# Finer waits, later weight loads, bf16 bound matmuls and a split last block in a transformer layer on 8 cores

## The reference

```python
lat = rmsnorm(x @ wkv_a_w.T, norm_w)
kv = lat @ wkv_b_w.T                     # k, v, split by heads; q = x @ wq_w.T
scores = jnp.einsum('bqhd,bkhd->bhqk', q, k) * scale      # causal mask
o = jnp.einsum('bhqk,bkhd->bqhd', softmax(scores), v)
return o @ out_w.T + out_b
```

## Time and profile before

| | us |
|---|---|
| runs of the kernel | 1611.94, 1614.55, 1836.63 (median 1614.55) |
| the profiled execution | 1611.35 |
| its slowest core, first to last instruction | 1609.5 |
| its quickest core | 1601.5 |

### The profile page before, as it was taken

How to read it: one execution, slowest core, us unless ns; L and a number is a source line. 1 busy time by engine, 2 the same in 40 slices (tenths; PEclk the granted TensorE clock), 3 DMA queues, 4 the chain that set the end, 5 groups by cost and what they waited for, 6 DMA issues and landing times.

```text
span 1609.5 us, 22614 instructions; the slowest of 8 cores (1601.5 to 1609.5 us)
## 1 busy us (share of the span) xinstructions
PE 1562.8 (97%) x8698; PEld 760.1 (47%) x8698; DVE 440.6 (27%) x996; ACT 363.4 (23%) x480; POOL 82.1 (5%) x174
## 2 busy tenths in 40 slices
PE   3999999999989999999999999999999999999998
PEld 2644555555554444444444444444444444444444
DVE  5735444444445662111111111011111111111111
ACT  3854565656652001101111001111011000000000
POOL 1210100000000000000000000000000000000000
PEclk8999999999999999999999999999999999999999
DMA  9853445222447975344653645473532283939110
GB/s 274 285 96 77 72 80 87 44 34 41 72 67 106 234 210 120 32 42 37 53 52 32 61 41 51 40 62 31 42 37 27 21 111 60 123 53 128 55 53 27
DMA packets 75607, 127.59 MB, mean 79 GB/s; under 512 B 46128, under 2 KB 48496, under 8 KB 70768
## 3 DMA queue, kind: packets, MB, share of 16 engines
q0 software_dynamic: 17856, 58.73, 35.5%
q1 hardware_dynamic: 57648, 67.42, 15.0%
HBM read 233.08 MB, written 16.78 MB: 155 GB/s over the span
## 4 chain that ended last, share of the span: by engine, by line
PE 92%; DMA 5%; DVE 1%; issue 1%; ACT 0%; POOL 0%; SPq 0%; DVEq 0%; ACTq 0%; POOLq 0%
PE PS L1324 21%; PE PS L1302 21%; PE PS L1308 21%; PE PS L1096 7%; PE PS L1284 4%; PE PS L1177 4%; PE PS L1153 4%; PE PS L1105 3%; PE PS L1115 3%; PE PS L1060 3%; DMA RES<-xq 2%; DMA WST<-wkva 1%; DMA OT<-ONa 1%; DMA X<-xq 1%; PE PS L1124 1%
## 5 line engine op out<-in xcount | busy, mean ns | idle before, releaser
L1302 PE MATMUL PS<-X2T,W 128*128 128x512 bf16 x1536 | 347.2, 379 | 0.0
L1308 PE MATMUL PS<-X2T,W 128*128 128x512 bf16 x1536 | 347.2, 379 | 0.0
L1308 PEld LDWEIGHTS PS<-X2T,W 128*128 128x128 fp8e4 x1536 | 150.3, 98 | 181.2
L1302 PEld LDWEIGHTS PS<-X2T,W 128*128 128x128 fp8e4 x1536 | 150.3, 98 | 181.2
L864 DVE SCALAR_TENSOR_TENSOR FUSE<-PS,CF,SIL 128x512 bf16<-128x512 f32 x96 | 72.1, 751 | 587.4 <-PE PS L1308 587.4
L1015 ACT ACTIVATE SIL<-PS,CF 128x512 bf16<-128x512 f32 x96 | 66.0, 687 | 589.7 <-PE PS L1302 589.6
L940 ACT ACTIVATE P<-PS,NEGB 128x1024 bf16<-128x1024 f32 x192 | 169.8, 899 | 124.8 <-PE PS L1153 115.7
L1324 PE MATMUL PS<-WDa,FUSE 128*128 128x512 fp8e4 x768 | 166.1, 379 | 0.0
L1324 PE MATMUL PS<-WDb,FUSE 128*128 128x512 fp8e4 x768 | 166.1, 379 | 0.0
L1324 PEld LDWEIGHTS PS<-WDa,FUSE 128*128 128x128 bf16 x768 | 75.1, 98 | 90.6
L1324 PEld LDWEIGHTS PS<-WDb,FUSE 128*128 128x128 bf16 x768 | 75.1, 98 | 90.6
(11 more groups left out here) (123 smaller groups left out, 956.4 us busy)
## 6 DMA issues: line engine op xcount, KB each, us to landing
W<-gu POOLq DMA_DIRECT2D x48, 512.0 KB, 8.3
WQ<-wq POOLq DMA_DIRECT2D x16, 512.0 KB, 6.6
X<-xo SPq DMA_DIRECT2D x8, 1024.0 KB, 9.1
WO<-wo POOLq DMA_DIRECT2D x16, 512.0 KB, 11.2
RES<-xq SPq DMA_DIRECT2D x8, 1024.0 KB, 6.8
res_scr<-RES SPq DMA_DIRECT2D x8, 1024.0 KB, 8.7
RB<-res_scr SPq DMA_DIRECT2D x32, 256.0 KB, 4.9
out<-OB SPq DMA_DIRECT2D x32, 256.0 KB, 2.5
```

The costliest lines, as they stand in the source:

```text
L1302: mm = e.matmul(bank(ffn_bank(f)), W8[io % 4][:, c * 128:(c + 1) * 128], X2T[:, c * 1024 + qb * 512:c * 1024 + qb * 512 + 512], start=(c = ...
L1308: mm = e.matmul(bank(ffn_bank(f) + 1), W8[io % 4][:, 2048 + c * 128:2048 + (c + 1) * 128], X2T[:, c * 1024 + qb * 512:c * 1024 + qb * 512 ...
```

## The change

1. P's waits for transposed heads: the first chunk waits for head 12 (208) instead of head 14 (240); chunks 13, 14 and 15 then wait for their own head.
2. W8[i], i = 0 to 3, waits for v_add of 8 + 4 i, that is for the adds of tiles 1, 2, 3 and 4.
3. NM and DG become bf16, and X and Y use the bf16 identity and ones. NEGB is multiplied by 1 + 2^-7, so that the bound stays one after the rounding.
4. The last down block (m = 31) is computed in two parts, columns 0 to 383 in bank 7 and 384 to 511 in bank 6, each with its own 48 matmuls, multiply, add and store. The second part waits until block 30 has left bank 6 (v_out 31).

```diff
-    NM = small("NM", 2)
+    NM = small("NM", 2, BF16)
...
-    DG = small("DG", 2)
+    DG = small("DG", 2, BF16)
...
+        e.wait_ge(v_out, 32)
+        e.dma_start(out=out_d.ap()[896:1024, 1536:1536 + CUT], in_=OB[1][:, 0:CUT]).then_inc(d_ob[1], 16)
+        e.wait_ge(v_out, 33)
+        e.dma_start(out=out_d.ap()[896:1024, 1536 + CUT:2048], in_=OB[1][:, CUT:512]).then_inc(d_end, 16)
+        e.wait_ge(d_end, 16)
...
         e.wait_ge(t_av, 192)
         for i in range(4):
+            e.wait_ge(v_add, 8 + 4 * i)
             e.dma_start(out=W8[i][:, :], in_=gu_d.ap()[i, :, :]).then_inc(d_gu[i], 16)
...
-                e.tensor_scalar(NEGB[:, h % 2:h % 2 + 1], YT[:, 0:1], -0.5 * SS, None, Op.mult).then_inc(v_y, 1)
+                e.tensor_scalar(NEGB[:, h % 2:h % 2 + 1], YT[:, 0:1], -0.5 * SS * ROUND_UP, None, Op.mult).then_inc(v_y, 1)
...
-            chain(e.tensor_mul(OB[m % 3][:, :], bank(6 + m % 2), DSC[:, db * 512:(db + 1) * 512]))
-            e.wait_ge(d_rb[m % 4], 16 * (m // 4 + 1))
-            e.tensor_add(OB[m % 3][:, :], OB[m % 3][:, :], RB[m % 4][:, :]).then_inc(v_out, 1)
+            for part, (b, lo, hi) in enumerate([(7, 0, CUT), (6, CUT, 512)] if m == 31 else [(6 + m % 2, 0, 512)]):
+                e.wait_ge(t_d, m + 1 + part)
+                chain(e.tensor_mul(OB[m % 3][:, lo:hi], bank(b, lo, hi), DSC[:, db * 512 + lo:db * 512 + hi]))
+                e.wait_ge(d_rb[m % 4], 16 * (m // 4 + 1))
+                e.tensor_add(OB[m % 3][:, lo:hi], OB[m % 3][:, lo:hi], RB[m % 4][:, lo:hi]).then_inc(v_out, 1)
...
-                mm = e.matmul(PS[0:2, b * 512:b * 512 + 128], NM[:, 0:2], IDF, start=True, stop=True)
+                mm = e.matmul(PS[0:2, b * 512:b * 512 + 128], NM[:, 0:2], IDB, start=True, stop=True)
...
-                mm = e.matmul(bank(b, 0, 2), ONEF[0:2, 0:128], DG[0:2, 0:2], start=True, stop=True)
+                mm = e.matmul(bank(b, 0, 2), CB[0:2, 128:256], DG[0:2, 0:2], start=True, stop=True)
...
-                if lo == 0 and d == 0:
-                    e.wait_ge(d_heads[0], 240)
                 for c in range(lo, lo + n):
-                    if d == 0 and c == 15:
-                        e.wait_ge(d_heads[0], 256)
+                    if d == 0 and c in (0, 13, 14, 15):
+                        e.wait_ge(d_heads[0], 16 * max(13, c + 1))
...
+            for part, (b, lo, hi) in enumerate([(7, 0, CUT), (6, CUT, 512)] if m == 31 else [(6 + m % 2, 0, 512)]):
+                if part == 1:
+                    e.wait_ge(v_out, 31)
+                for c in range(48):
+                    if m == 0 and c == 46:
+                        e.wait_ge(v_fuse, 94)
+                    mm = e.matmul(bank(b, lo, hi), FUSE[:, c * 1024 + t * 128:c * 1024 + (t + 1) * 128],
+                                  WD[db % 2][:, c * 512 + lo:c * 512 + hi], start=(c == 0), stop=(c == 47))
+                mm.then_inc(t_d, 1)
```

More of the change, by code:

```diff
@@ L18 @@
 SQRT_MAGIC = 0x1FBD1DF5
+ROUND_UP = 1.0 + 2.0 ** -7
 VW = 130
@@ L129, in first_plan @@
             (v(12), 4), (v(13), 6), (("N", 0), 7), (v(14), 4), (("X", 0), 6), (v(15), 5), (("Y", 0), 7)]
+CUT = 384
 UNITS = {"Q": 16, "K": 4, "V": 4, "N": 3, "X": 1, "Y": 1, "P": 16}
@@ L310, in build_nc @@
     d_ob = [sem(f"d_ob{i}") for i in range(3)]
+    d_end = sem("d_end")
     v_chain = sem("v_chain")
@@ L531, in sync_prog @@
                             in_=OB[q % 3][:, :]).then_inc(d_ob[q % 3], 16)
-        for q in range(29, 32):
+        for q in range(29, 31):
             e.wait_ge(v_out, q + 1)
@@ L869, in vector_prog @@
             db, t = divmod(m, 8)
-            e.wait_ge(t_d, m + 1)
             if m >= 3:
                 e.wait_ge(d_ob[m % 3], 16 * (m // 3))
-            chain(e.tensor_mul(OB[m % 3][:, :], bank(6 + m % 2), DSC[:, db * 512:(db + 1) * 512]))
-            e.wait_ge(d_rb[m % 4], 16 * (m // 4 + 1))
-            e.tensor_add(OB[m % 3][:, :], OB[m % 3][:, :], RB[m % 4][:, :]).then_inc(v_out, 1)
+            for part, (b, lo, hi) in enumerate([(7, 0, CUT), (6, CUT, 512)] if m == 31 else [(6 + m % 2, 0, 512)]):
[3 more added lines that the diff above has]
+                e.tensor_add(OB[m % 3][:, lo:hi], OB[m % 3][:, lo:hi], RB[m % 4][:, lo:hi]).then_inc(v_out, 1)
     def scalar_prog(e):
```

## The result

The changed kernel takes 1604.42 us (median of 5 runs), the kernel before 1614.55 beside it: a ratio of 0.9943 with an interval of 0.9931 to 0.9955, 9.2 us gained where 16.4 were forecast. That is within 2%, as forecast. The time is 8.4 us above the forecast and 0.4 us above the top of the range. Executions in which a whole die ran at a lower clock are in these two medians, which without them are 1603.8 and 1612.9, and are left out of every ratio, median, range and count from here on.

What follows compares the result with a forecast made beforehand. TensorE, busy for 1562.8 of 1609.5 us, was taken as the bound. Edits 1 to 4 at 1.5 + 4.5 + 9.8 + 0.6 = 16.4 us off 1611.35 gave 1595.0, plus 1: 1596 us, own range 1591 to 1600.

Steps and rivals of the forecast that it cites:

- Edit 3: bf16 X and Y matmuls in the heads: 0.65 us saved in each of 15 heads, 9.8 us, bounds 8.3 to 11.3.
- what was taken to be left of the 0.84 us a head: X and Y in a steady head: two small matmuls plus issue, 0.09 to 0.29 us left, 0.19 taken.
- Rival B: X and Y in the heads: bf16 removes only one instruction of each two; 5 us less gain, 1601 us, chance 0.15.
- signs named ahead: Right: one X and one Y a head, under 0.3 us together; wrong: X or Y of 0.2 us or more.
- Edit 1: Head 15: P's 8.0 us wait goes, a shorter one comes at step 4's values; 1.5 us gained, bounds 0 to 9.7.
- The 1.7 us of cold clock: Head 15: the new idle time may cost 1.7 us of lower clock, leaving 1.2 of 2.9 us gained.
- Rival A: Head 15: nothing replaces P's wait, so all 9.7 us come; 8.2 us more gain, 1588 us, chance 0.12.
- Edit 2: Projection: the 2.8 us wait for RES and 1.7 us of cold clock go; 4.5 us gained, bounds 0 and 4.5.
- rival D: Residual rounds: held-back weight loads collide with spills, X2T transposes and RES loads; slower than before, 1625 us, chance 0.03.
- can hold a transpose up by 6.5 us only: Residual rounds: one weight load, 9 packets an engine, delays an X2T transpose by at most 6.5 us.
- Edit 4: Last down block in two parts: shorter final multiply and add, no store gain; net 0.6 us, bounds -0.3 and 3.
- C: Projection: RES2 stays late behind the head's transpose in SP's queue; 4.5 us less gain, 1601 us, chance 0.07.

Runs made afterwards that it cites:

- doubled matmuls: Changed kernel with each X and each Y matmul issued twice in a row: 1603.0 us in one run.
- the two remedies: Changed kernel with the first tile's residual add moved to steps 6 to 9 of head 15 (1595.38 us), or with the last WO load held back (1599.9 us).
- edit 2 alone: Kernel before with only W8[0..3] waiting for the adds of tiles 1 to 4: 1611.4 us, ratio 0.9999.
- the residual later: Changed kernel with the first residual tile's bias added in steps 6 to 9 of head 15 instead of 2 to 5: 1595.38 us, ratio 0.9917.
- the two kernels with WO held back: Changed kernel with the last four WO loads waiting for head 14's first transpose: 1599.9 us; the same with the first residual tile's bias later: 1603.2 us.
- weights start behind a transpose, or early: W8 waiting for X2T transposes: on before 1608.7 us, on changed with residual later 1596.53, two tiles sooner 1596.2; residual later with W8 loads right after the last values: 1599.78.
- the first two groups: Runs on two chips, each with the kernel before beside them: the four edits alone (before 1612.57 us); the head 15 and doubled-matmul kernels (before 1611.52 us).
- edits 1, 3 and 4 alone: Kernel before with only the finer head waits (1611.53 us), only the bf16 X and Y (1608.45 us), or only the split last block (1611.43 us).
- the three kernels with the later start: W8 loads waiting for X2T transposes of tiles 3 to 6, on before (1608.7 us) or changed with residual later (1596.53); the latter two tiles sooner (1596.2).

## Why the forecast was off

**What bounds it.** Right: TensorE is busy for 1562.5 us, and each edit paid only by taking work out of it, idle time out of it, or what comes after.

**Edit 3, the step that failed.** 9.8 us forecast, 5.2 measured, 4.0 alone: 4.6 of the 7.2 us that were missed. The step that failed is what was taken to be left of the 0.84 us a head: 0.19, where 0.47 stays. The price of 0.84 holds the 0.11 behind X and behind Y, and the rest of 0.19 ("0.09 to 0.29") holds no such term: it was struck out with fp32, though the trace of after still has it behind both bf16 matmuls. That is 0.22 of the 0.28 that were missed; the other 0.06 is the start, about 0.09 and 0.07 us where 0.05 each was taken. The matmuls' own prices, 0.057 and 0.031, were right, as the doubled ones show. With 0.47 left, 15 x 0.37 = 5.6, near the measured 5.1. Rival B was close, with 4.7: of each two instructions one is left, X at 0.15, half of 0.31, and Y at 0.10. The signs named ahead did not tell the two apart, since X and Y together are 0.25, under the 0.3 named as right. Of the 5.1, bf16 alone gives back another 1 us behind the heads.

**Edit 1, the wait right, the clock not.** The new wait stands at the named instruction, with the named releaser, and 2.24 us after `residual` began, where 2.2 was the step. Of 1.5 us forecast none came on the two slowest cores (27.2 and 27.4), and 1.7 on the mean of the four later cores (28.2 and 26.5). The doubled matmuls, the same order of head 15 once more, have 28.4 to 29.0 on theirs, so what the edit brings lies between nothing and 2 us, and the 1.5 is not refuted. Its working is. The 1.7 us of cold clock were charged as a new loss, but the kernel before lost about 1.4 there already, so that core 7's 2.1 is only 0.7 more. And four short waits that the 8.0 had covered were left out: of the first values for ONa (1.1), for NEGB (1.2), for ONb (0.9) and for the exponentials (0.3). With the 3.6 us they make 7.2 of waiting, 0.8 less than 8.0, and the clock takes nearly all of that. Alone the edit gives 0.5, not clear of nothing. Rival A's 9.7 was out of reach with this order, and the two remedies show how much was: from 27.4 to 21.9 on the slowest cores.

**Edit 2, right where it was looked at, wrong about its price.** The wait for RES is gone on all cores and the projection went from 108.1 (core 6) to 103.4 (cores 0 to 3), 4.7 for 4.5. In the profiled execution of after 2.6 of it were lost on die 1 to a dip of the clock (below). What failed is the sentence against rival D, "can hold a transpose up by 6.5 us only": a transpose of 13 us was stretched to 35.6 beside one load. It is D's collision, a weight load beside an X2T transpose, but one core at a time and in some runs, and with engines that nearly stop, not with 152 packets that each wait their turn. Counting runs whose slowest core stands 4.7 us or more above the next (a line drawn after the runs were seen), it shows in 4 of 10 runs of edit 2 alone, in 1 of 7 with the residual later, in 3 of 6 and 4 of 6 of the two kernels with WO held back, in none of 4 of the changed kernel and not in the one with doubled matmuls: 12 of 34. Where weights start behind a transpose, or early, it shows in 0 of 29. In the four runs of the changed kernel the slowest core is at most 2.6 us above the next, so it is no part of its 1604.4.

**Edit 4, too small.** 0.6 forecast, 1.0 in the trace, 1.1 to 1.5 alone. The multiply and add measured 0.29 each, nearly as taken (0.31), and the second part 2.7 us, as taken. The forecast put the store's gain at 0, since the transfers it looked at took the same time "whatever they move", though the earlier trace rows has 6.8 us for 1024 KB; with a quarter of the bytes it landed 0.5 us sooner. The rule of the Trainium skill that spoke against the edit (TensorE: Matmul & The Clock Gate, "Back-to-back issue gap", about 81 ns a pair in a sustained stream) is not borne out here: the 48 pairs of the second part take 2.68 us, 56 ns each, and the edit gained.

**The sum.** Of the 7.2 us that were missed, edit 3 is 4.6. The other 2.6 can't be given to one edit: edit 1 brought between nothing and 2 us of 1.5, and edit 2 brought 2.1 of 4.5 along the slowest cores of the profiled executions. With the residual later, core 3 of that version against core 6 of before shows all terms at once: 5.2 (heads), 5.6 (head 15), 4.7 (projection), 1.0 (end), 16.5 together. So 16.4 was the gain of a kernel with one more edit, and by other terms: half of edit 3's, nearly four times edit 1's. That the two numbers meet is luck.

**The range** was too narrow below its middle by one term: its top was rival B or C alone, plus 3, while edit 3's price and, in the profiled execution, edit 1's short waits, the late first X (1.9 us) and the dip of the clock (2.6) all went one way.

## What to carry to other kernels

Before a wait is loosened, follow the in-order queue of the engine behind it to the next instruction that wants the same late data, and move that one too; here this was worth 5.6 us, and the wait alone 0.5 by ratio. Before a loss is charged to a change, look whether the kernel before has it in the same place, as with the clock here. Price a small matmul that stands alone behind a semaphore by a lone one, with what follows it (0.26 us for X and 0.21 for Y), and not by its like in a run. Where a converting weight load and large DMA transposes meet, try a load that waits for the transpose in flight: here that cost some 1 us at most against the best runs, and no run with it was among the ones up to 16 us longer.

## What the runs showed of the hardware

**DMA engines that are busy and hardly move.** The pair of a converting load and a transpose fell to 27 to 33 GB/s for 10 us on one core, at a time when core 1 moved 283 with the same pair. That edit 2's start of the loads brings it is shown: within the first two groups, 12 of 30 runs with such a start have a lone core, and none of 68 without it (the kernel before, and edits 1, 3 and 4 alone). That the later start cures it is likely, not shown: 0 of 29, but all on other chips, where edit 2 as it was did not run. An overlap as such does not bring it: in the traces of the three kernels with the later start a load and the next transpose overlap too, for 1 to 7 us. Slow transposes are commoner than lone cores: 28.8 us on core 5 with the residual later, a core as quick as its like (1593.1, the slowest 1593.3). Why it strikes one core in one run and not another is open: no trace has rows from inside the DMA engines.

**A clock that dips on a whole die.** In after's profiled execution cores 4 to 7 were granted less than 1.00 three times, near 508, 558 and 573 us, with TensorE busy nearly throughout; cores 0 to 3 were not. TensorE's windows of core 4, core 7, and core 0:

```profile
570.00:576.00 6.00, 5.91 (x25) 0.85 1.03 288
```

```profile
556.00:562.00 6.00, 6.00 (x25) 0.84 1.00 194
570.00:576.00 6.00, 6.00 (x25) 0.85 1.03 211
```

```profile
570.00:576.00 6.00, 6.00 (x29) 1.00 1.09 319
```

25 matmuls instead of 29 in 6 us; the projection is 2.6 us longer on each of the four cores (106.0 for 103.4). In windows of 2 us the clock reads 0.81, between the 1.2 GHz and 2.4 GHz levels. The projection of the doubled matmuls, which have all four edits, has no such dip (103.3 to 103.4 on all cores), nor has edit 2 alone, so it belongs to an execution and not to an edit. The Trainium skill, TensorE: Matmul & The Clock Gate, Part 1, tells of a current limiter that takes a whole die to 13/16 once three of its cores run dense matmuls, and holds it while the load lasts. The figure and the reach fit the dips; the rest does not fit this execution, since its eight cores run dense matmuls all along at a mean clock of 0.990 to 0.999.
